# Attention's first keys, values and mask table loaded during the stage before it, and the last stores of that stage awaited by one engine

## Chip, cores and metric

One Trainium2 chip, one NeuronCore. The time is that of one execution of the program on the device, in microseconds; the kernel before was run three times.

## What is computed

Two layers of a small transformer-like network on x of shape (2, 2048, 256) in float32:

```python
x = L0_attn(x)      # a second-order linear recurrence along the sequence: B_mat in, scan, C_mat out, + x * D
x = L0_ffn(x)       # products with the signs of a 256x256 matrix, scale, bias, clip to +-100
# both between layer norms and residuals
x = L1_attn(x)      # 16 heads of 16, ALiBi slopes, causal softmax(Q K^T / 4) V, then W_out
x = L1_ffn(x)       # rotary attention with 4 key/value heads for 16 query heads, then 8 experts, top 2, SwiGLU
```

Only the two causal attentions and what comes just before them matter here. The kernel runs both in one stage of 16 steps, four heads of one batch and one attention in each step.

## The kernel before

The program is a row of stages, each with its own block of instruction streams for the five engines; a block ends when all its engines have ended.

**front** (to about 85 us) loads x, normalises it and runs the recurrence. SyncE's queue loads constants too (L147 to L163), among them the mask pieces `fill` and `after`, which count on the semaphore `s_masks`.

**middle** (to 321 us) works through 8 blocks of 512 tokens, 0 to 3 of the first batch and 4 to 7 of the second (`both(blk, ...)`). For each block it projects queries, keys and values for both attentions, splits queries and keys into a high and a low part (seven tiles `part[m]`: ScalarE's `high(m)` at L797 and L800, VectorE's `low(m)` at L907 and L910), and SyncE stores everything to DRAM: rows of x (L595, L596), `part[0..3]` as `qa_parts` and `ka_parts`, values `va_tiles` (L600), `part[4..6]` as `qb_parts` and `kb_parts` (L606), and `vb_tiles` last (L609). Buffers are reused: ScalarE's `high(m)` waits on `s_pst[m]` for the store of the block before, VectorE's value copy (L942) waits on `s_vst` for `va_tiles` and `vb_tiles` of the block before. The orders of all engines are written out by hand.

The first attention step (t = 0) reads batch 0 only, so its operands are complete in DRAM after block 3. GpSimd therefore loads part of them while the middle still runs (L533 to L585): `x_rows(blk)` and `carry(blk + 1)` for the middle itself, at block 5 a wait for the stores of block 3, then one third of the queries per block (`first_queries`, six loads of 256 KB into `q0`), and at the end `first_extras` and `first_keys`, which fill `k0a`, the keys of the first 512 tokens alone (six loads of 64 KB and two of 24 KB). SyncE closes the middle with waits for all stores of all seven parts, of the rows and of the values, and for `s_first`.

**attention** (from 325 us) runs the 16 steps. Work units of a step stand in a string written by hand, `FIRST_ORDER` for step 0: `m` is a max tile (TensorE L1406, reduced by VectorE at L1574 or L1577), `r` turns a block's row maxima on TensorE (L1433), `w` copies them (ScalarE) and SyncE stores them into two rows of `q` (L1258), `s` is a score tile (L1417, masked by L1383, exponential on ScalarE L1524), `v` a value product (L1485), `t`, `d`, `o` handle the output. Step 0 begins with 17 max tiles, then `r`, `w`, one more `m`, and the first `s`. Seven PSUM banks go round among m, r, s and t tiles, so that the tile in a bank waits for the reader of the tile seven before.

At the stage's start SyncE loads the mask table `later` (256 KB, L1263) and the keys of tokens 512 to 1023, and ScalarE the keys of tokens 1024 to 2047 and the values of step 0 (1 MB). TensorE and VectorE wait for `s_masks` = 64, so for `later`; TensorE waits for the further keys where they are first used, and issues ten dense products that do nothing but keep it busy before the first `r`:

```python
            pe.wait_ge(M["s_masks"], 64)
...
                        if t == 0 and n == 2 * KEYED[0]:
                            pe.wait_ge(s_k[0], NFK)
                        if t == 0 and n == 2 * KEYED[1]:
                            pe.wait_ge(s_k[1], NFK)
...
                        if t == 0 and n == 0:
                            keep_going(pe, M, ps_o, 10)
```

The later stages (output projections, routing, experts) are not touched.

Of the kernel before, what the change touches and what calls it, by code (L numbers as in the profile page):

```python
# [9 lines left out]
F32 = mybir.dt.float32  # L10
# [3 lines left out]

P = 128
# [72 lines left out]
def front(nc, A, M):  # L88
# [5 lines left out]
    with ExitStack() as ctx:  # L94
# [47 lines left out]
        def _(sp):  # L142
# [14 lines left out]
            for dst, src in ((M["fill"], "c_fill"),  # L157
                             (M["after_q"][0], "c_after0"), (M["after_q"][1], "c_after1")):
                sp.dma_start(dst[:, :], A[src]).then_inc(M["s_masks"], 16)
# [281 lines left out]
def first_keys(eng, M, j):  # L441

    for n in range(NPROD):
        at = HALF * j + n * HD
        eng.dma_start(M["k0a"][at:at + HD, :, :].bitcast(F32),
                      M["ka_d"][PROD_K[n], 0:GH * HD, 0:BT].rearrange("(p j d) t -> j d p t", p=PAIRS, j=2)[j]
                      ).then_inc(M["s_first"], 16)
    at = HALF * j + DOTS
    eng.dma_start(M["k0a"][at:at + SLOPED + 2, :, :].bitcast(F32),
                  M["aug_d"][SLOPED:2 * SLOPED + 2, j * PAIRS:(j + 1) * PAIRS, 0:BT]).then_inc(M["s_first"], 16)  # L450


def first_extras(eng, M, j):
    at, heads = HALF * j + DOTS, slice(j * PAIRS, (j + 1) * PAIRS)
    eng.dma_start(M["q0"][at:at + SLOPED, :, :].bitcast(F32), M["aug_d"][0:SLOPED, heads, :]).then_inc(M["s_first"], 16)


def middle(nc, A, M):

    with ExitStack() as ctx:  # L460
# [68 lines left out]
        def _(pool):  # L529
# [41 lines left out]
            for blk in range(2, NBLK):  # L571
# [15 lines left out]
        def _(sp):  # L587
# [3 lines left out]
            for blk in range(NBLK):  # L591
# [5 lines left out]
                for m in range(NS):  # L597
                    if m == 4:
# [8 lines left out]
                                 part[m][:, :, :].bitcast(F32)).then_inc(s_pst[m], 16)  # L607
                sp.wait_ge(s_va, blk * 2 + 2)
# [420 lines left out]
KEYED = [min(m for m in range(NMX) if MAXES[m][2][0][2] >= k0) for k0 in (WIDE, 2 * WIDE)]  # L1029
# [63 lines left out]
def attention(nc, A, M):  # L1093
# [4 lines left out]
    with ExitStack() as ctx:  # L1098
# [7 lines left out]
        q_op = [M["q0"], *(sb(f"a_q{i}", [P, PAIRS, L], F32R) for i in range(1, 3))]  # L1106
        v_op = [sb(f"a_v{i}", [P, KT, GH * VW]) for i in range(3)]
        prob = sb("a_p", [P, NPB, QB])
        fill, after_q = M["fill"], M["after_q"]
        later = sb("a_later", [P, WIDE])  # L1110
# [9 lines left out]
        numbers = sb("a_numbers", [P, TOK // P])  # L1120
        raw_w = sb("a_raww", [P, WIDE], F32R)
        high_w = sb("a_highw", [P, WIDE], F32R)
        k_op = [sb(f"a_k{i}", [P, PAIRS, L], F32R) for i in (0, 2, 1)]
        k_op = [k_op[0], k_op[2], k_op[1]]
# [6 lines left out]
        s_k = [sem(f"att_first_keys_loaded{i}") for i in range(2)]  # L1131
        s_v = [sem(f"att_values_loaded{i}") for i in range(5)]
# [23 lines left out]
        DIRECT = 2  # L1156
        TOPS = NQB - DIRECT
# [76 lines left out]
        NFK = (2 * NPROD + 2) * 16  # L1234

        def first_step_keys(eng, done, lo, hi):

            for j in range(2):
                for n in range(NPROD):
                    at = HALF * j + n * HD  # L1240
                    eng.dma_start(k_op[0][at:at + HD, :, lo:hi].bitcast(F32),
                                  M["ka_d"][PROD_K[n], 0:GH * HD, lo:hi].rearrange(
                                      "(p j d) t -> j d p t", p=PAIRS, j=2)[j]).then_inc(done, 16)
                at = HALF * j + DOTS
                eng.dma_start(k_op[0][at:at + SLOPED + 2, :, lo:hi].bitcast(F32),
                              M["aug_d"][SLOPED:2 * SLOPED + 2, j * PAIRS:(j + 1) * PAIRS, lo:hi]).then_inc(done, 16)

# [3 lines left out]
        def _(sp):  # L1251
# [11 lines left out]
            sp.dma_start(later[:, :], A["c_later"]).then_inc(M["s_masks"], 16)  # L1263
            first_step_keys(sp, s_k[0], BT, 2 * BT)
# [25 lines left out]
        def _(pool):  # L1290
            pool.sem_inc(s_mp, MP0)
            nc.gpsimd.memset(zeros[:, :, :], 0.0).then_inc(s_hi, 1)
            pool.dma_start(numbers[:, :], A["c_ids"]).then_inc(s_zs, 16)
            pool.wait_ge(s_hi, 1)
            pool.wait_ge(s_zs, 16)
# [41 lines left out]
            def step(t):  # L1337
# [3 lines left out]
                for what, h in work_of(t):  # L1341
# [7 lines left out]
                    elif t == 0 and what == "max" and n % 5 == 0 and 0 <= n // 5 - 4 < len(LOADS):  # L1349
                        pool.wait_ge(s_mt, 2 * n)  # L1350
# [14 lines left out]
            pool.wait_ge(s_zs, 16 + HSROWS // P // FILL * 16)  # L1365
# [3 lines left out]
        def _(pe):  # L1369
            pe.sem_inc(s_tt, TT0)  # L1370
            pe.sem_inc(s_rt, RT0)
            pe.wait_ge(M["s_masks"], 64)
# [14 lines left out]

            def keys_of(r, k0):

                return M["k0a"] if r == 0 and k0 < BT else k_op[r % 3]  # L1390
# [9 lines left out]
            def max_half(r, n, bank):  # L1400
# [3 lines left out]
                for p, qt, k0, w, col in MAXES[n // 2 % NMX][2]:  # L1404
                    kp = 0 if r >= NGB else p
                    ins = pe.matmul(ps[bank][:, col:col + w], q_op[r % 3][part, p, qt * P:(qt + 1) * P],  # L1406
                                    keys_of(r, k0)[part, kp, k0:k0 + w], start=True, stop=True)
                ins.then_inc(s_mt, 1)

            def score_half(r, n, bank):  # L1410
# [4 lines left out]
                for p, kt, c0, w, col in tiles:  # L1415
                    kp = 0 if r >= NGB else p
                    ins = pe.matmul(ps[bank][:, col:col + w], keys_of(r, kt * P)[part, kp, kt * P:(kt + 1) * P],  # L1417
# [19 lines left out]
            def step(t):  # L1437
                o = t % 3
                for what, n in work_of(t):
                    bank = BANKS[t].get((what, n))  # L1440
                    if what == "max":
                        if t == 0 and n == 2 * KEYED[0]:
                            pe.wait_ge(s_k[0], NFK)
                        if t == 0 and n == 2 * KEYED[1]:
                            pe.wait_ge(s_k[1], NFK)
# [5 lines left out]
                    elif what == "rows":  # L1451
                        if t == 0 and n == 0:
# [1068 lines left out]
```

## Time and profile before

| | |
|---|---|
| three runs | 2369.0, 2370.15, 2374.59 us; median 2370.15 us |
| the profiled execution | 2369.36 us, its span 2367.5 us |
| TensorE busy | 2178.2 us, 92% of the span |
| VectorE busy | 2031.6 us, 86% |
| ScalarE busy | 1546.6 us, 65% |
| GpSimd busy | 674.4 us, 28% |
| mean granted TensorE clock | 0.962 of full speed |

Times in the rows are microseconds from the start of the span. PE is TensorE, PEld its weight loads, DVE VectorE, ACT ScalarE, POOL GpSimd, SP SyncE; a q behind the name (SPq) marks an instruction that issues a DMA. "[11.80 <-DMA ...]" is the idle time of the engine before the row, and what ended it. PEclk is the granted TensorE clock, 1.00 for 2.4 GHz and 0.50 for 1.2 GHz. A DMA share is the mean busy share of the 16 DMA engines (it can read a little above 1).

### The profile page before, as it was taken

The numbers are of one execution on the slowest core, as the hardware profiler recorded it, in microseconds if no ns is written. First come the engines' busy times: TensorE is split into PE (matmuls) and PEld (weight loads), VectorE is DVE, ScalarE is ACT, GpSimd is POOL, SyncE is SP. The second block draws the span as 40 slices with busy tenths as digits, with TensorE's granted clock in tenths as the row PEclk, the third lists the DMA queues.
The fourth block names the chain that finished last, engine by engine and source line by source line (L and its number), as shares of the span: only waits on it lengthen the run. The fifth ranks groups of instructions, "written<-read, shape, count | busy, mean of one in ns | idle before, by whom it ended". The sixth has DMA issues, their size and how long they took to land. (4 is left out here: it accounts for less than half of the span.)

```text
span 2367.5 us, 47823 instructions
## 1 busy us (share of the span) xinstructions
PE 2178.2 (92%) x15794; PEld 1265.1 (53%) x15795; DVE 2031.6 (86%) x5155; ACT 1546.6 (65%) x3005; POOL 674.4 (28%) x999
## 2 busy tenths in 40 slices
PE   4599968999999999999999999999998885999997
PEld 2355544444444444444444444444444653888886
DVE  7799958999999999999999999999991664777775
ACT  3144414678888888888888888888886542455443
POOL 5523002232322322322322322322111353333333
PEclk8799977999999999999999999999999996999999
DMA  4179875664554554342442442443133885444443
GB/s 168 58 221 266 275 172 80 115 123 89 103 109 89 100 112 89 82 91 66 82 90 66 83 89 66 83 88 75 53 89 108 292 280 200 81 82 80 80 80 69
DMA packets 176844, 273.63 MB, mean 116 GB/s; under 512 B 53656, under 2 KB 126504, under 8 KB 170804
## 3 DMA queue, kind: packets, MB, share of 16 engines
q0 software_dynamic: 45984, 137.68, 28.7%
q1 hardware_dynamic: 125620, 123.13, 17.3%
q10 hardware_dynamic: 5044, 10.32, 1.5%
q8 instruction: 109, 1.79, 0.3%
q14 instruction: 87, 0.71, 0.1%
HBM read 128.77 MB, written 141.24 MB: 114 GB/s over the span
## 5 line engine op out<-in xcount | busy, mean ns | idle before, releaser
L1524 ACT ACTIVATE a_p<-banks 128x512 f32<-128x512 f32 x2176 | 1131.3, 609 | 257.1 <-PE banks L1417 206.5
L1577 DVE TENSOR_REDUCE a_mx<-banks 128x1 f32<-128x512 f32 x1536 | 944.1, 682 | 19.1 <-PE banks L1406 19.0
L1485 PE MATMUL banks<-a_p,a_v 128*32 128x512 f32 (+3 forms) x5120 | 588.9, 544 | 1.5 <-ACT a_o L1542 1.1
L1406 PE MATMUL banks<-a_k,a_q 52*128 52x512 f32 (+5 forms) x1600 | 446.8, 413 | 1.9 <-DVE a_rowtop L1574 0.3
L1417 PE MATMUL banks<-a_q,a_k 50*128 50x512 f32 (+7 forms) x1600 | 415.9, 396 | 1.1
L1574 DVE CUSTOM_DVE_ANT_0 a_masked<-banks,a_later 128x512 bf16<-128x512 f32 (+3 forms) x768 | 331.0, 485 | 20.3 <-PE banks L1406 18.4
L1417 PEld LDWEIGHTS banks<-a_q,a_k 54*128 54x128 f32 (+1 forms) x1600 | 227.1, 185 | 199.0 <-DVE a_mx L1577 95.6
L1406 PEld LDWEIGHTS banks<-a_k,a_q 52*128 52x128 f32 (+1 forms) x1600 | 224.1, 185 | 117.9 <-DVE a_mx L1577 55.4
L1406 PE MATMUL banks<-a_k,q 48*128 48x512 f32 (+6 forms) x896 | 256.5, 419 | 6.1 <-DMA a_k<-aug_rows 4.6
L1417 PE MATMUL banks<-q,a_k 50*128 50x512 f32 (+7 forms) x896 | 231.2, 400 | 1.2 <-DVE a_orow L1597 0.3
L1485 PEld LDWEIGHTS banks<-a_p,a_v 128*32 128x32 f32 x5120 | 109.3, 108 | 175.0 <-issue 125.9
L2173 POOL DMA_INDIRECT out_rows<-e_y,e_token x72 | 113.2, 1572 | 260.3 <-DMA out_rows<-e_y,e_token 218.2
L1417 PEld LDWEIGHTS banks<-q,a_k 50*128 50x128 f32 (+1 forms) x896 | 125.1, 187 | 115.4 <-DVE a_mx L1577 46.4
L2207 PE MATMUL banks<-w,e_hT 128*128 x576 | 170.6, 398 | 3.1 <-DVE e_hT L2315 3.1
L1406 PEld LDWEIGHTS banks<-a_k,q 48*128 48x128 f32 (+1 forms) x896 | 128.9, 189 | 71.1 <-DVE a_mx L1577 30.1
L1383 PE MATMUL banks<-fill,after 64*128 64x128 bf16 (+1 forms) x1280 | 132.2, 213 | 0.0
L1574 DVE CUSTOM_DVE_ANT_0 a_masked<-banks,a_later,a_mx 128x384 bf16<-128x384 f32 (+3 forms) x256 | 127.4, 545 | 2.5 <-PE banks L1406 2.1
L2281 ACT ACTIVATE e_w<-w 128x1024 fp32r x72 | 76.4, 1061 | 77.5 <-PE banks L2227 77.4
L2227 PE MATMUL banks<-e_w,e_gT 128*128 128x256 f32 x864 | 121.4, 290 | 0.7 <-DVE e_y L2348 0.7
L2207 PEld LDWEIGHTS banks<-w,e_hT 128*128 128x128 f32 x576 | 104.2, 190 | 23.5 <-issue 4.0
L1333 POOL TENSOR_TENSOR a_mpart<-a_rowtop,a_zeros 128x16 fp32r<-128x16 f32 x64 | 14.6, 229 | 341.3 <-DVE a_rowtop L1581 320.4
L2263 ACT ACTIVATE e_hT<-banks 128x256 fp32r<-128x256 f32 x72 | 27.6, 384 | 126.0 <-PE banks L2194 99.5
(279 smaller groups left out, 2983.6 us busy)
## 6 DMA issues: line engine op xcount, KB each, us to landing
expert_rows<-a_zeros POOLq DMA_DIRECT2D x132, 258.0 KB, 5.3
a_k<-ka_parts POOLq DMA_DIRECT2D x42, 256.0 KB, 6.3
e_x<-expert_rows SPq DMA_DIRECT2D x72, 129.0 KB, 2.2
expert_rows<-e_y SPq DMA_DIRECT2D x72, 128.0 KB
qa_parts<-m_part SPq DMA_DIRECT2D x16, 512.0 KB, 6.5
ka_parts<-m_part SPq DMA_DIRECT2D x16, 512.0 KB, 5.4
va_tiles<-m_va SPq DMA_DIRECT2D x8, 1024.0 KB, 6.8
qb_parts<-m_part SPq DMA_DIRECT2D x16, 512.0 KB
```

The lines of the kernel that those rows point to most:

```text
L1383: ins[j] = pe.matmul(blocks[:, :, HALF * n:HALF * (n + 1)], steps[n][half, :], fill[half, :].unsqueeze(1).to_broadcast([HALF, len(at), HALF]),
L1406: ins = pe.matmul(ps[bank][:, col:col + w], q_op[r % 3][part, p, qt * P:(qt + 1) * P], keys_of(r, k0)[part, kp, k0:k0 + w], start=True, st ...
L1417: ins = pe.matmul(ps[bank][:, col:col + w], keys_of(r, kt * P)[part, kp, kt * P:(kt + 1) * P], q_op[r % 3][part, p, qb * QB + c0:qb * QB + ...
L1485: ins = pe.matmul(ps_o[VW * h:VW * h + VW, c0:c0 + w], v_op[o][:, kt, hk * VW:hk * VW + VW], prob[:, (at + slot) % NPB, col:col + w], star ...
L1524: nc.scalar.activation(prob[:, (t * NSC + n) % NPB, :], ps[bank][:, :], ACT.Exp, scale=SCALE).then_inc(s_ex, 1)
L1574: ins = v.tensor_tensor_reduce(masked[:, j, col:col + w], ps[bank][:, col:col + w], later[:, WIDE - w:WIDE], 1.0, least, ALU.add, ALU.max, ...
L1577: ins = v.tensor_reduce(top, ps[bank][:, :], AX.X, ALU.max)
L2173: pool.indirect_dma_start(out=out, out_offset=bass.IndirectOffsetOnAxis(ap=token[n % R][:, :], axis=0), in_=y[n % R][:, :], in_offset=None ...
L2207: ins = pe.matmul(bank[:, :], hT[c][s][:, k, :], of[:, ds(at, 1), part * FFN:(part + 1) * FFN].rearrange("p o m -> p (o m)"), start=(k == ...
L2227: ins = pe.matmul(ps_y[:, 0:D], gT[c][s][:, f, :], w2p[of][s][:, f, :], start=(f == 0 and c == 0 and of == 0), stop=(f == FT - 1 and c == 1))
L2263: nc.scalar.activation(hT[0][s][:, :, :].rearrange("p k t -> p (k t)"), ps_h[:, 0:D], ACT.Copy).then_inc(s_hi, 1)
L2281: nc.scalar.activation(w2p[0][s][:, :, :], w2[:, ds(e * FT, FT), :], ACT.Copy)
```

## The change

Batch 0's half of `xnT` and of `f2` are no longer read once block 3 has gone through, and the full keys (`k0`, 2 MB) and the values (`v0`, 1 MB) of step 0 are placed there. `first_keys` loads full keys by thirds beside the queries, `first_values` is a new load in SyncE's queue before the last store of block 5, `later` and `numbers` are loaded in front. The loads at attention's start, the waits on `s_k` and the dense products before the first `r` are gone. The middle no longer waits for its last stores of parts and values; GpSimd does, before its first load for step 1.

```diff
             for dst, src in ((M["fill"], "c_fill"),
+                             (M["later"], "c_later"), (M["numbers"], "c_ids"),
                              (M["after_q"][0], "c_after0"), (M["after_q"][1], "c_after1")):
                 sp.dma_start(dst[:, :], A[src]).then_inc(M["s_masks"], 16)
...
-def first_keys(eng, M, j):
-    for n in range(NPROD):
-        at = HALF * j + n * HD
-        eng.dma_start(M["k0a"][at:at + HD, :, :].bitcast(F32),
-                      M["ka_d"][PROD_K[n], 0:GH * HD, 0:BT].rearrange("(p j d) t -> j d p t", p=PAIRS, j=2)[j]
-                      ).then_inc(M["s_first"], 16)
...
+def first_keys(eng, M, j, n):
+    at = HALF * j + n * HD
+    eng.dma_start(M["k0"][at:at + HD, :, :].bitcast(F32),
+                  M["ka_d"][PROD_K[n], 0:GH * HD, :].rearrange("(p j d) t -> j d p t", p=PAIRS, j=2)[j]
+                  ).then_inc(M["s_first"], 16)
+
+def first_values(eng, M):
+    eng.dma_start(M["v0"][:, :, :], M["va_d"].rearrange("(k p) c -> p k c", p=P)[:, 0:KT, 0:GH * VW]
+                  ).then_inc(M["s_first_values"], 16)
...
 def first_extras(eng, M, j):
...
+    eng.dma_start(M["k0"][at:at + SLOPED + 2, :, :].bitcast(F32),
+                  M["aug_d"][SLOPED:2 * SLOPED + 2, heads, :]).then_inc(M["s_first"], 16)
...
                 if blk == NBB + 1:
-                    for m in range(2):
+                    for m in range(4):
                         pool.wait_ge(s_pst[m], NBB * 16 + 16)
                 if blk > NBB:
                     for j in range(2):
                         first_queries(pool, M, j, blk - NBB - 1)
+                        first_keys(pool, M, j, blk - NBB - 1)
             for j in range(2):
                 first_extras(pool, M, j)
-                first_keys(pool, M, j)
...
+                if blk == NBB + 1:
+                    sp.wait_ge(s_vst, NBB * 32 + 16)
+                    first_values(sp, M)
                 sp.wait_ge(s_va, blk * 2 + 2)
                 sp.dma_start(vb_d[:, blk * TPB:(blk + 1) * TPB, :],
                              vb[:, :, :, :].rearrange("p j h c -> p j (h c)")).then_inc(s_vst, 16)
-            for m in range(NS):
-                sp.wait_ge(s_pst[m], NBLK * 16 + 16)
             for i in range(2):
                 sp.wait_ge(s_st[i], NBLK // 2 * 32 + 16)
-            sp.wait_ge(s_vst, NBLK * 32 + 16)
             sp.wait_ge(M["s_first"], NFIRST)
+            sp.wait_ge(M["s_first_values"], 16)
...
-            sp.dma_start(later[:, :], A["c_later"]).then_inc(M["s_masks"], 16)
-            first_step_keys(sp, s_k[0], BT, 2 * BT)
...
-            first_step_keys(act, s_k[1], 2 * BT, L)
-            load(act, 0, ("values", 0, 0))
...
+                        if n // 5 == 4:
+                            for done, count in zip(M["s_moved"], M["moved"]):
+                                pool.wait_ge(done, count)
                         pool.wait_ge(s_mt, 2 * n)
                         load(pool, 1, LOADS[n // 5 - 4])
...
-                        if t == 0 and n == 2 * KEYED[0]:
-                            pe.wait_ge(s_k[0], NFK)
-                        if t == 0 and n == 2 * KEYED[1]:
-                            pe.wait_ge(s_k[1], NFK)
...
-                        if t == 0 and n == 0:
-                            keep_going(pe, M, ps_o, 10)
```

Waits for `s_masks` = 64 become waits for 80. In attention the buffers are laid out anew, so that `k0` and `v0` keep their places and the others go around them.

## Rows read from the trace of the kernel before

**Rows 1.** The page: busy time of each engine and its share of the span

```profile
PE 2178.2 (92%) x15794; PEld 1265.1 (53%) x15795; DVE 2031.6 (86%) x5155; ACT 1546.6 (65%) x3005; POOL 674.4 (28%) x999
```

**Rows 2.** Busy time by stretch, from the middle's end into attention's first step

```profile
318.00:321.50 3.50, 0.27 (x3) 0.08 (x1) 1.66 (x4) 0.63 (x1) 0.00 (x0) 1.00 0.43 135
...
321.50:345.30 23.80, 10.63 (x38) 7.54 (x39) 11.37 (x45) 0.00 (x0) 1.69 (x5) 0.50 0.84 147
345.30:352.20 6.90, 3.92 (x31) 2.48 (x31) 2.36 (x4) 2.96 (x4) 0.00 (x0) 0.99 0.01 2
352.20:365.90 13.70, 13.68 (x66) 7.12 (x64) 12.29 (x36) 3.25 (x6) 0.38 (x1) 0.50 0.00 1
...
386.30:444.40 58.10, 52.16 (x351) 24.11 (x350) 53.03 (x141) 31.24 (x60) 16.83 (x30) 0.94 0.72 118
```

**Rows 3.** Timeline of SyncE's DMA queue at the end of the middle (start us, issue us)

```profile
320.24 0.79 SPq L609 DMA_DIRECT2D vb_tiles<-m_vb  x1
325.54 0.35 SPq L1263 DMA_DIRECT2D a_later<-in_c_later  x1
```

**Rows 4.** DMA issues, 290 to 345 us: size, median us from issue to landing

```profile
a_later<-in_c_later SPq DMA_DIRECT2D x1, 256.0 KB, 4.5
...
vb_tiles<-m_vb SPq DMA_DIRECT2D x1, 256.0 KB, 4.6
```

**Rows 5.** Timeline of TensorE at attention's start: start us, us, [idle before <- releaser]

```profile
330.08 6.58 PE L1406 MATMUL banks<-k0a,q 52*128 52x384 f32 x20 [11.80 <-DMA a_later<-in_c_later]
341.25 0.80 PE L1406 MATMUL banks<-a_k,q 52*128 52x384 f32 x4 [4.59 <-DMA a_k<-aug_rows]
...
342.50 3.85 PE L75 MATMUL banks<-ident 128*128 128x128 f32 x20
346.19 0.60 PE L1433 MATMUL banks<-ident,a_mpart 128*8 128x128 f32 x4
...
350.19 0.51 PE L1417 MATMUL banks<-q,k0a 54*128 54x512 f32 x2 [2.98 <-DMA q<-a_mrow]
```

**Rows 6.** Timelines of VectorE, then GpSimd, at attention's start

```profile
331.06 0.56 DVE L1574 CUSTOM_DVE_ANT_0 a_masked<-banks,a_later 128x384 bf16<-128x384 f32 x1 [11.25 <-PE banks L1406]
...
338.16 0.21 POOL L1335 TENSOR_TENSOR a_mpart<-a_rowtop,a_mpart 128x16 fp32r<-128x16 f32 x1
```

**Rows 7.** Busy time by stretch in the second half of the middle; last: clock, DMA, GB/s

```profile
217.00:220.00 3.00, 2.61 (x24) 2.61 (x25) 2.90 (x5) 2.12 (x4) 1.98 (x3) 1.00 0.98 197
223.00:226.00 3.00, 3.00 (x8) 1.33 (x7) 2.82 (x6) 2.16 (x4) 0.00 (x0) 1.00 0.69 245
226.00:265.00 39.00, 38.89 (x149) 23.19 (x148) 35.04 (x82) 17.13 (x43) 7.33 (x13) 1.00 1.04 316
...
265.00:277.00 12.00, 12.00 (x48) 6.64 (x46) 11.29 (x20) 6.67 (x12) 0.00 (x0) 1.00 0.43 141
```

**Rows 8.** Timeline of GpSimd in the middle: the first load for attention

```profile
211.01 1.05 POOL L436 DMA_DIRECT2D q<-qa_parts  x2 [28.73 <-DMA qa_parts<-m_part]
```

**Rows 9.** Timeline of VectorE in the middle: values of three blocks taken

```profile
234.84 1.41 DVE L942 TENSOR_TENSOR m_va<-banks,m_bv 128x256 f32<-128x256 f32 x4
...
259.87 1.41 DVE L942 TENSOR_TENSOR m_va<-banks,m_bv 128x256 f32<-128x256 f32 x4
...
284.91 1.41 DVE L942 TENSOR_TENSOR m_va<-banks,m_bv 128x256 f32<-128x256 f32 x4
```

**Rows 10.** Timeline of SyncE's DMA queue in the middle: the three stores before those

```profile
225.68 0.61 SPq L609 DMA_DIRECT2D vb_tiles<-m_vb  x1
...
251.28 0.52 SPq L609 DMA_DIRECT2D vb_tiles<-m_vb  x1
...
275.48 0.78 SPq L609 DMA_DIRECT2D vb_tiles<-m_vb  x1
```

**Rows 11.** DMA issues, 251 to 252 us, then 232 to 234 us: us to landing

```profile
vb_tiles<-m_vb SPq DMA_DIRECT2D x1, 256.0 KB, 7.7
...
qa_parts<-m_part SPq DMA_DIRECT2D x1, 512.0 KB, 16.5
```

More of the change, by code:

```diff
@@ L13 @@
 ds = bass.ds
+SBUF_START, SBUF_END = 16512, 229344
+F32_BYTES, BF16_BYTES = 4, 2
 P = 128
@@ L156, in _ @@
             sp.dma_start(aug[:, :], A["c_aug"]).then_inc(s_aug, 16)
-            for dst, src in ((M["fill"], "c_fill"),
+            for dst, src in ((M["fill"], "c_fill"), (M["later"], "c_later"), (M["numbers"], "c_ids"),
                              (M["after_q"][0], "c_after0"), (M["after_q"][1], "c_after1")):
@@ L1105, in attention @@
         ps, ident = M["ps"], M["ident"]
-        q_op = [M["q0"], *(sb(f"a_q{i}", [P, PAIRS, L], F32R) for i in range(1, 3))]
-        v_op = [sb(f"a_v{i}", [P, KT, GH * VW]) for i in range(3)]
+        sb("a_room_k0", [P, PAIRS, L], F32R)
+        q1 = sb("a_q1", [P, PAIRS, L], F32R)
+        sb("a_room_v0", [P, KT, GH * VW])
+        v_op = [M["v0"], *(sb(f"a_v{i}", [P, KT, GH * VW]) for i in range(1, 3))]
         prob = sb("a_p", [P, NPB, QB])
         fill, after_q = M["fill"], M["after_q"]
-        later = sb("a_later", [P, WIDE])
+        later, numbers = M["later"], M["numbers"]
         masked = sb("a_masked", [P, 2, WIDE], BF16)
@@ L1119, in attention @@
         zeros = sb("a_zeros", [P, FILL, DR])
[L1120 removed]
         raw_w = sb("a_raww", [P, WIDE], F32R)
         high_w = sb("a_highw", [P, WIDE], F32R)
[L1123 to L1124 removed]
+        q_op = [M["q0"], q1, sb("a_q2", [P, PAIRS, L], F32R)]
+        k2, k1 = sb("a_k2", [P, PAIRS, L], F32R), sb("a_k1", [P, PAIRS, L], F32R)
+        k_op = [M["k0"], k1, k2]
         ps_o = ps[RING]
@@ L1130, in attention @@
         s_q = [M["s_first"], *(sem(f"att_operands_loaded{i}") for i in range(1, 5))]
-        s_k = [sem(f"att_first_keys_loaded{i}") for i in range(2)]
-        s_v = [sem(f"att_values_loaded{i}") for i in range(5)]
+        s_v = [M["s_first_values"], *(sem(f"att_values_loaded{i}") for i in range(1, 5))]
         s_mt = sem("att_max_tile_scored")
@@ L1232, in load @@
                               va_d[:, ds(b * KT, KT), ds(g * GH * VW, GH * VW)]).then_inc(v_sem, 16)
[L1234 to L1246, printed above, removed]
         block = ctx.enter_context(nc.Block())
@@ L1371, in _ @@
             pe.sem_inc(s_rt, RT0)
-            pe.wait_ge(M["s_masks"], 64)
+            pe.wait_ge(M["s_masks"], NMASKS)
             def mask(outs, tiles, steps):
@@ L1406, in max_half @@
                     ins = pe.matmul(ps[bank][:, col:col + w], q_op[r % 3][part, p, qt * P:(qt + 1) * P],
-                                    keys_of(r, k0)[part, kp, k0:k0 + w], start=True, stop=True)
+                                    k_op[r % 3][part, kp, k0:k0 + w], start=True, stop=True)
                 ins.then_inc(s_mt, 1)
@@ L1550, in _ @@
             ch = Chain(dve, s_dve)
-            dve.wait_ge(M["s_masks"], 64)
+            dve.wait_ge(M["s_masks"], NMASKS)
             dve.sem_inc(s_te, TE0)
@@ L2406, in of_both @@
                 return early.enter_context(nc.sbuf_tensor(name, shape, dt))
-            M["k0a"] = of_both("k0a", [P, PAIRS, BT], F32R)
+            M["later"] = of_both("later", [P, WIDE], F32)
+            M["numbers"] = of_both("numbers", [P, TOK // P], F32)
             M["q0"] = of_both("q0", [P, PAIRS, L], F32R)
@@ L2412, in program @@
             M["s_masks"], M["s_first"] = nc.alloc_semaphore("masks_loaded"), nc.alloc_semaphore("first_operands")
+            M["s_first_values"] = nc.alloc_semaphore("first_values")
             with ExitStack() as first:
```

21 lines of the change are left out of this document (9 added, 12 removed).

## The prediction, before the run

> **What bounds the kernel now.** I read the page first [rows 1]: TensorE is busy for 92% of the span, VectorE for 86%, and nearly all of that is the 16 attention steps, which the change leaves alone. So I went to the only place that the diff touches, the seam between the middle and attention, and read it by stretch [rows 2]. TensorE does nothing from 318.3 us on; the granted clock is 1.00 up to 321.5 us and 0.50 (1.2 GHz) from there to 345.3 us. Then the timelines [rows 3, 5, 6]. Two waits in a row end last there. SyncE's last store (`vb_tiles`) is issued at 320.24 us and lands 4.6 us later [rows 3, 4], at 324.8; the next stage's first instruction on SyncE comes at 325.54, so the block change costs 0.7 us. That instruction is the load of the mask table, 4.5 us to land [rows 4], at 330.04, and TensorE's first max tile starts at 330.08 [rows 5]. Later come an idle stretch of 4.59 us for further keys, 3.85 us of dense filler products, and a wait for the stored row maxima; the first score tile starts at 350.19 [rows 5]. Everything after is a chain of TensorE and VectorE work in a fixed order, so what is saved before 350.19 should be saved at the end.
>
> **The seam, step by step.** (1) Stores of parts and values are no longer awaited in the middle. What ends it next is SyncE's issue of the last one, 320.24 + 0.79 = 321.03 [rows 3]; with the same 0.7 us for the change of block, attention begins at 321.7 instead of 325.5. The stores are awaited by GpSimd before its first load for step 1, at max tile 20, well past the first score, so after they have landed: nothing. (2) The mask table is already there, as are keys and values: TensorE starts at once, at 321.8, which is 8.3 us earlier than 330.08. (3) From VectorE's first tile to the first score the kernel took 350.19 - 331.06 = 19.1 us [rows 5, 6]. GpSimd had the parts of the first row maxima ready at 338.16 + 0.21, that is 7.3 us after VectorE's start [rows 6], and TensorE turned them only at 346.19, because the keys (4.59 us idle) and the filler (3.85 us) stood before it in its queue. With both gone TensorE reaches the turn when the ring of seven banks lets it issue the 17th max tile, which is after VectorE's tenth tile, at about the same 7.3 us. From the turn to the first score stay 350.19 - 346.19 = 4.0 us. So 11.4 us in place of 19.1: 7.7 us. The first of VectorE's further tiles cover most of those 4 us. The sum of the seam is 8.3 + 7.7 = 16.0 us. (4) Removing the filler also removes what preceded the short full-clock stretch of 345.3 to 352.2 [rows 2]; TensorE was busy there for 3.9 us, 0.8 of it the filler, and without it some 2 us of real work may run at half clock. Bounds 0 (it waits for the store anyway) and 2 us; I take 1. Seam: 15 us gained. (5) Two more DMAs in front (256 and 16 KB) and the reordered `s_masks` loads are under the recurrence, which uses no DMA to speak of; the removed issues of SyncE and ScalarE at attention's start kept nobody waiting. Nothing. Were the cover in front gone, the table would cost its 4.5 us [rows 4].
>
> **The price in the middle.** The loads do not vanish, they move to where DMA is busy. From 226 to 265 us the 16 DMA engines are at 1.04, full, at 316 GB/s; before that, 223 to 226, at 0.69, and afterwards, 265 to 277, at 0.43 [rows 7]. TensorE is busy for 38.9 of those 39 us and VectorE for 35.0, so a stall there is not absorbed. The new key loads are 6 x 256 + 2 x 96 KB in place of 6 x 64 + 2 x 24 KB, 1.33 MB more. Loads of this kind run slowly even alone: 197 GB/s with the engines at 0.98 in 217 to 220 us [rows 7], where they are nearly all there is. At that rate the surplus is 6.7 us of all engines; at 316 GB/s it would be 4.2. I take 6.7, the row of the same kind of load, less the 0.9 us free in 223 to 226: the backlog grows by 5.8 us. Also GpSimd's wait at 211.01 [rows 8] now includes the stores of keys, which SyncE issues after those of queries; I allow 3 us for that. With two more loads to issue at 0.5 us each [rows 8], the two middle operations queued behind, `x_rows(6)` and `carry(7)`, come some 4 us later. Their readers are two blocks away; nothing.
>
> Who waits for the backlog? VectorE's copy of values waits for the `vb_tiles` store of the block before, the last store in each block. For block 5 it was issued at 251.28 and landed 7.7 us later, at 258.98 [rows 10, 11]; the copy began at 259.87 [rows 9]. There is 0.9 us of room. With the store 5.8 us later, VectorE stalls for 4.9 us, perhaps split between this block and the one before (store issued 225.68, copy at 234.84 [rows 9, 10]). Behind VectorE's wait stand the rope of the block, and TensorE waits for that copy to free its banks. VectorE regains its own wait for TensorE after the copy, about 1 us: 4 us lost. Then the values: `first_values`, 1 MB in pieces of 512 bytes, goes into SyncE's queue right before the `vb_tiles` store of block 5 (issued 275.48; the copy that needs it at 284.91 [rows 9, 10]). That store used to be down 4.5 to 5 us after its issue, so 4.5 us of room. 1 MB at 316 GB/s is 3.3 us, at 197 it is 5.3: a stall of 0 to 1.5 us with the issue itself; I take 1. Together **5 us** lost in the middle; the bounds are 0 (all of it fits into gaps) and about 11.
>
> A row and a rule differ on how it is spread. A 512 KB store of queries issued while GpSimd's loads held the engines took 16.5 us to land [rows 11], where a load or store of the middle otherwise takes 5 to 8; it looked as if whoever had queued first was served first. The Trainium skill (DMA: Bandwidth & Descriptors, "Queues, rings and completion order") says instead that each DMA engine takes turns between the queues that have work, packet by packet. By turns, with GpSimd's packets the larger ones, SyncE's stores would crawl for as long as GpSimd has loads; that is the second rival.
>
> **Sum.** 15 - 5 = 10 us from the profiled execution's 2369.36 us: 2359.4. The median of the three runs is 0.8 us above that execution, within their spread, and I give **2359.5 us**.
>
> **Rivals.** *Transfers fit after all* (chance 0.20): the larger loads may move at the 316 GB/s of the mixed stretch, and the 12 us at 0.43 after 265 us [rows 7] speak for room; against it the full engines from 226 us. Then the seam's 15 us stand alone: 2354.4 us. *Stores held out by GpSimd's loads* (0.22): GpSimd now has 12 x 256 KB of operands, 2 x 512 KB of x and 0.33 MB of extras from about 216.5 us on, 4.5 MB, at 197 GB/s 23 us, and with the gap before `x_rows(7)` it would be done at about 243. The `vb_tiles` store issued at 225.68 then lands there and not at 230.3; the copy wanted at 234.84 stalls for 8 us. With 1.5 us for the values 9.5 us are lost: 2363.9 us. The store of 16.5 us speaks for it; against it, the store issued at 251.28 took only 7.7 us though the engines were just as full. *The clock stays down* (0.07), which ends slower: with no filler before the first `r`, step 0's thin max tiles might leave TensorE at 1.2 GHz until about 444 us. At 0.50 it did 66 products in 13.7 us (4.8 per us), in 386.3 to 444.4, near full clock, 355 in 58.1 (6.1 per us) [rows 2]; at the lower rate those 355 take 74 us in place of 58, 16 us more: 2375 us, and beyond if it lasts into step 1. It decides from the point at which the clock is still at 0.50 past 430 us. Against it, that same stretch of 386.3 to 444.4 has nearly full clock with no filler near it. The Trainium skill (TensorE: Matmul & The Clock Gate, "Part 1: The HAM clock gate") calls the throttled state the default that activity releases, which speaks against taking filler away; by it alone I would not know when the clock returns. *The change doesn't do what it says* (0.03): something else, such as late first operands, holds the block change; 2369.
>
> **Numbers.** The forecast has 0.48. About 0.3% (7 us) can be told from no change, so faster means below 2363.0. Forecast 0.42 + first rival 0.20 + the better end of the second 0.05 = 0.67 faster; slower 0.06; the rest, 0.27, the same. The forecast's own range is 2355 to 2364; the first rival with its bounds reaches down to 2351, the second with its bounds to 2367. Range 2351 to 2367.
>
> **What the changed profile would show.** Right: attention's first TensorE product 3.5 us after the middle's last one, no idle time for the table or keys, first score 11 to 12 us after VectorE's first tile; in the middle a VectorE wait of 2 to 6 us before L942 released by a DMA at block 4 or 5, blocks of 25.0 us grown by 5 in all. Wrong: no wait before L942 (first rival); one of 8 us at block 4 (second); clock 0.50 in the 400 us (third). Most would be wrong with the forecast if the middle's delay were above 8 us, or if the first score were reached later than 335 us plus that delay.

## The result, and the profile after

The changed kernel takes **2382.38 us** (median of six runs, 2379.91 to 2385.51), the kernel before in the same comparison 2371.82 us (2368.81 to 2375.6). The ratio is 1.0039 [1.0024, 1.0054]: about 0.4% slower, where I had forecast 0.45% faster. The profiled execution took 2385.51 us, its span 2383.7 us, its mean granted clock 0.953.

The page, busy time of each engine, answers to [rows 1]:

```profile
PE 2184.8 (92%) x15774; PEld 1268.6 (53%) x15775; DVE 2031.6 (85%) x5155; ACT 1547.0 (65%) x3005; POOL 673.8 (28%) x998
```

VectorE does the same work to a tenth of a microsecond, and TensorE only 6.6 us more, so the time is in waits and in the clock. For the place, I set VectorE's instructions beside each other: every kernel of this study has the same 5155 in the same order, so the k-th of one can be held against the k-th of the other. The delay of the changed kernel is +22.2 us at the end of the middle, +13.9 at attention's first max tile, +7.3 at the first tile behind the first score, +13.8 at 465 us, +14.0 at attention's end and +16.2 at the end of the program. So the middle loses 22.2 us, the seam gives back 14.9, 6.5 are lost early in step 0, 0.2 in the rest of attention and 2.2 in the stages behind it, which no kernel changes and where the profiles of this study differ from that of before by 3.8 us more to 2.7 us less. The profiled execution is 3.1 us above its median, and that of before 2.5 us below the 2371.82 of the comparison, which is why the profiles are 16.2 us apart and the medians 10.6.

**The middle.** Busy time by stretch (columns as in [rows 7]: PE, PEld, DVE, ACT, POOL, then clock, DMA share, GB/s):

```profile
218.00:224.00 6.00, 6.00 (x20) 2.96 (x20) 5.69 (x8) 2.26 (x4) 5.82 (x7) 1.00 0.96 107
232.00:240.00 8.00, 7.25 (x30) 4.55 (x28) 2.62 (x6) 2.86 (x10) 2.41 (x5) 1.00 1.03 228
240.00:250.00 10.00, 0.00 (x0) 0.00 (x0) 0.00 (x0) 0.00 (x0) 0.00 (x0) 0.64 1.07 168
```

For ten microseconds no engine computes, and the DMA engines are full at 168 GB/s. The timeline of VectorE, then of TensorE, names the wait:

```profile
258.35 1.42 DVE L959 TENSOR_TENSOR m_va<-banks,m_bv 128x256 f32<-128x256 f32 x4 [23.72 <-DMA vb_tiles<-m_vb]
...
259.15 3.78 PE L679 MATMUL banks<-m_hT,m_wb 128*128 128x512 f32 x4 [19.90 <-DVE m_va L959]
```

It is the copy of values that [rows 9] show at 234.84 us, and it waits for the store of block 3. Timeline of SyncE's queue, then the DMA issues of 225.2 to 225.5 us:

```profile
225.21 0.52 SPq L628 DMA_DIRECT2D vb_tiles<-m_vb  x1
...
227.59 23.81 SPq L622 DMA_DIRECT2D qa_parts<-m_part  x2
...
vb_tiles<-m_vb SPq DMA_DIRECT2D x1, 256.0 KB, 33.1
```

The store was issued 0.5 us earlier than before and landed 33.1 us later, at 258.3. Behind it SyncE itself sat 23.81 us in the issue of the next stores. The queues of 228 to 256 us (packets, MB, share of the 16 engines' time) show who held the engines:

```profile
q0 software_dynamic: 654, 2.95, 57.0%
q1 hardware_dynamic: 2182, 2.79, 45.9%
```

q0 is GpSimd's queue, q1 SyncE's. In 218 to 224 us q0 had them nearly alone (94.0%). The packets of that stretch:

```profile
DMA packets 126, 0.64 MB, mean 107 GB/s; under 512 B 43, under 2 KB 43, under 8 KB 54
```

72 of the 126 are of 8 KB or more: all but one of them are rows of 2048 tokens of queries and keys, 8 KB each, into 16 partitions.

**The seam.** Timelines of TensorE, VectorE, GpSimd and SyncE around attention's start answer to [rows 3, 5, 6]:

```profile
342.48 0.79 SPq L628 DMA_DIRECT2D vb_tiles<-m_vb  x1
343.93 0.53 POOL L1294 MEMSET a_zeros<- 128x516 f32 x1 [109.53 <-POOLq L476]
344.34 8.17 PE L1406 MATMUL banks<-k,q 52*128 52x384 f32 x25 [3.82 <-PEq L476]
345.01 0.56 DVE L1566 CUSTOM_DVE_ANT_0 a_masked<-banks,later 128x384 bf16<-128x384 f32 x1 [2.96 <-PE banks L1406]
352.48 1.01 PE L1433 MATMUL banks<-ident,a_mpart 128*8 128x128 f32 x4
356.92 0.80 PE L1417 MATMUL banks<-q,k 54*128 54x512 f32 x2 [2.60 <-DVE a_mx L1569]
```

The last store is issued at 343.27 and the block changes 0.66 us later; no operand is waited for; the first score comes 11.9 us after VectorE's first tile.

**Step 0's clock.** Busy time by stretch from attention's start; in the kernel before, the clock was 0.94 in 386.3 to 444.4 us [rows 2]:

```profile
345.20:399.90 54.70, 47.23 (x218) 26.46 (x216) 43.90 (x126) 18.03 (x32) 5.28 (x12) 0.50 0.29 47
399.90:465.00 65.10, 59.28 (x361) 28.73 (x359) 56.04 (x150) 34.28 (x65) 18.61 (x33) 0.82 0.67 115
```

### The profile page after: what moved, and what is told of

Same layout as the page of the kernel before. It is cut to its first block and busy times, and to the rows that moved or that the text cites. A ratio compares the mean times of both kernels' runs of the same rounds, so it can differ in the third digit from the quotient of the medians.

```text
span 2383.7 us, 47767 instructions
## 1 busy us (share of the span) xinstructions
PE 2184.8 (92%) x15774; PEld 1268.6 (53%) x15775; DVE 2031.6 (85%) x5155; ACT 1547.0 (65%) x3005; POOL 673.8 (28%) x998
## 5 line engine op out<-in xcount | busy, mean ns | idle before, releaser
L1479 PE MATMUL banks<-a_p,a_v 128*32 128x512 f32 (+3 forms) x3200 | 364.6, 539 | 0.0
L1566 DVE CUSTOM_DVE_ANT_0 a_masked<-banks,later 128x512 bf16<-128x512 f32 (+3 forms) x768 | 330.9, 485 | 12.3 <-PE banks L1406 10.5
L1406 PE MATMUL banks<-k,q 52*128 52x512 f32 (+5 forms) x960 | 278.3, 435 | 5.4 <-PEq L476 3.8
L1417 PE MATMUL banks<-q,k 54*128 54x512 f32 (+5 forms) x960 | 258.1, 416 | 10.1 <-DMA q<-a_mrow 6.3
L1479 PE MATMUL banks<-a_p,v 128*32 128x512 f32 (+3 forms) x1920 | 227.5, 558 | 1.6 <-ACT a_o L1534 1.1
L1417 PEld LDWEIGHTS banks<-q,k 54*128 54x128 f32 (+1 forms) x960 | 139.8, 194 | 138.2 <-DVE a_mx L1569 52.4
L1406 PEld LDWEIGHTS banks<-k,q 52*128 52x128 f32 (+1 forms) x960 | 142.1, 197 | 78.8 <-DVE a_mx L1569 32.8
L1566 DVE CUSTOM_DVE_ANT_0 a_masked<-banks,later,a_mx 128x384 bf16<-128x384 f32 (+3 forms) x256 | 127.2, 543 | 0.6 <-PE banks L1406 0.2
L1479 PEld LDWEIGHTS banks<-a_p,a_v 128*32 128x32 f32 x3200 | 68.1, 108 | 105.9 <-issue 79.3
```

Of the source, the lines that this page charges most:

```text
L1417: ins = pe.matmul(ps[bank][:, col:col + w], k_op[r % 3][part, kp, kt * P:(kt + 1) * P], q_op[r % 3][part, p, qb * QB + c0:qb * QB + c0 + w ...
L1479: ins = pe.matmul(ps_o[VW * h:VW * h + VW, c0:c0 + w], v_op[o][:, kt, hk * VW:hk * VW + VW], prob[:, (at + slot) % NPB, col:col + w], star ...
L1566: ins = v.tensor_tensor_reduce(masked[:, j, col:col + w], ps[bank][:, col:col + w], later[:, WIDE - w:WIDE], 1.0, least, ALU.add, ALU.max, ...
```

## The experiments

Twelve kernels, in three groups of four, each group timed against the kernel before on one chip (its medians there: 2373.51, 2369.77 and 2368.7 us). Diffs are against the changed kernel unless another is named. "Delay" is always VectorE's, against the profile of before. All of them compute the full result. Kernels of different groups are compared by their ratios.

**e1, further keys late.** Only the keys of the first 512 tokens are loaded in the middle, as before; the others at attention's start. Barrier, mask table and values stay as changed.

```diff
-                        first_keys(pool, M, j, blk - NBB - 1)
             for j in range(2):
                 first_extras(pool, M, j)
+                for n in range(NPROD):
+                    some_keys(pool, M, j, n, 0, BT, M["s_first"])
...
+                    some_keys(sp, M, j, n, BT, 2 * BT, s_k[0])
...
+                            pe.wait_ge(s_k[0], 2 * NPROD * 16)
```

> The changed kernel, but only the keys of the first 512 tokens are loaded in the middle; the others at attention's start, by SyncE and ScalarE, and waited for as in the kernel before. Values, mask table and the awaited stores stay as changed. Theory 1 (GpSimd's full key loads hold SyncE's stores out of the DMA engines): VectorE's wait of 23.7 us before its copy of values falls below 2 us and the middle ends at 321 us as before; the first score comes some 8 us earlier than in the kernel before (keys are awaited again), and with 0 to 6 us given back in step 0 the time is 2364 to 2371 us. Theory 2 (the 1 MB of values in SyncE's queue, or the new order of SyncE's waits, makes the stall): it stays above 15 us and the time is 2380 us or more.

Measured: 2365.57 us, 0.9963 [0.995, 0.9976], as theory 1 had it. The middle's delay is +0.4 us instead of +22.2, so the larger key loads are what costs the middle its time. The first score comes 9.0 us earlier than before; TensorE waits for the further keys again, as its timeline shows:

```profile
334.87 1.33 PE L1412 MATMUL banks<-k,q 52*128 52x384 f32 x5 [6.08 <-DMA k<-ka_parts]
```

**e2, values late.** The 1 MB of values goes back to attention's start.

```diff
-                if blk == NBB + 1:
-                    sp.wait_ge(s_vst, NBB * 32 + 16)
-                    first_values(sp, M)
...
+            first_values(act, M)
```

> The changed kernel with one part undone: the values of step 0 are loaded by ScalarE at attention's start instead of by SyncE in the middle. Theory 1: nothing changes, VectorE's wait before its copy of values in the fifth block stays at 22 to 25 us, the time at 2380 to 2385 us. Theory 2: the wait goes and the time falls to 2362 or below.

Measured: 2379.95 us, 1.0035 [1.0022, 1.0047], theory 1 again; the middle's delay +21.0 us. The waits of 200 to 345 us (total, count, longest):

```profile
DVE m_va L955 <- DMA vb_tiles<-m_vb: 23.0, 1, 23.0
```

The values cost the middle 1.2 us of its 22.2. One thing more: the delay is +6.0 us at the first score and +6.2 at 465 us, so this profile does not show the 6.5 us that the changed kernel's lost there, with the same work.

**e3, queries and keys a third per block.** The loads stay GpSimd's, but each third waits until the values of its block are taken.

```diff
+            def paced(n):
+                pool.wait_ge(s_va, (NBB + n) * 2 + 1)
+                for j in range(2):
+                    first_queries(pool, M, j, n)
+                    first_keys(pool, M, j, n)
```

> The changed kernel with the same loads paced: GpSimd issues each third of queries and keys (1 MB) only when VectorE has just copied the values of blocks 4, 5 and 6, so that each burst has the 16 us until the next store that anyone waits for. Same bytes, same queues. Theory 1 with the point that it is the burst that holds stores out: the middle is longer by 0 to 3 us and the time is 2356 to 2364 us. Rival (the extra bytes cost DMA time wherever they stand): the middle is longer by 5 to 10 us, 2364 to 2372 us.

Measured: 2369.66 us, 0.998 [0.9971, 0.999]. The middle's delay falls to +7.6 us. VectorE's timeline shows where the rest is:

```profile
285.70 1.42 DVE L964 TENSOR_TENSOR m_va<-banks,m_bv 128x256 f32<-128x256 f32 x4 [1.47 <-DMA vb_tiles<-m_vb]
...
314.68 1.42 DVE L964 TENSOR_TENSOR m_va<-banks,m_bv 128x256 f32<-128x256 f32 x4 [9.07 <-DMA vb_tiles<-m_vb]
```

A third is still 1 MB at a time, and the last one, with the extras, falls on block 7's wait. Spreading helps by 14.6 us of 22.2, but the middle stays longer by what the rival said (5 to 10 us), not by 0 to 3: pacing alone is not enough.

**e4, e3 with the dense products back.**

```diff
+                        if t == 0 and n == 0:
+                            keep_going(pe, M, ps_o, 10)
```

> e3_paced with the ten dense filler products before the first turned rows put back. Theory 3 (their removal leaves TensorE at 1.2 GHz for most of step 0, which gave back 6.5 us between the first score and 465 us in the changed kernel): the first score comes up to 4 us later than in e3_paced, but step 0 gives back less, and the time is 0 to 4 us below e3_paced. Rival (the clock in step 0 does not hang on the filler): 2 to 4 us above e3_paced.

Measured: 2371.84 us, 0.9988 [0.9979, 0.9997]. Against e3 the first score is 5.1 us later, 2.2 us later at 465 us, and the median 2.18 us above: by these two profiles the products win back part of their cost in clock, not all. The time is where the rival had it, 2 to 4 us above e3; the intervals of the two ratios overlap.

**e5, keys of 1024 tokens early.** e1 with `0, 2 * BT` in the middle, and SyncE's loads and TensorE's first wait gone.

```diff
-                    some_keys(pool, M, j, n, 0, BT, M["s_first"])
+                    some_keys(pool, M, j, n, 0, 2 * BT, M["s_first"])
```

> e1_keys_late with the keys of tokens 512 to 1023 loaded in the middle too (six loads of 128 KB in place of 64 KB at the end of GpSimd's middle), only tokens 1024 to 2047 at attention's start. Theory 1 (what costs is the DMA time of loads into 16 partitions, about 8 us per MB of it, where stores are waited for): 0.4 MB more costs the middle 0 to 3 us, the wait for keys goes, and the first score comes 10 to 14 us earlier than in the kernel before; at 465 us 7 to 10 us are left; time 2361 to 2366 us. Rival: the room in the middle is used up already, the stall before the copy of values is above 5 us and the time is no better than e1_keys_late.

Measured: 2358.15 us, 0.9948 [0.9937, 0.996]. The middle's delay is -0.1 us with a VectorE wait of 1.0 us, the first score 14.6 us early and the end 14.2: the seam's whole gain at no price in the middle. The time is 3 us below the range expected: step 0 gave back 0.8 us, not 3 to 4.

**e6, all keys, by SyncE.** Two key loads stand in SyncE's own queue behind the values store in each of blocks 4, 5 and 6; queries stay with GpSimd, which no longer waits for the key stores.

```diff
+                    if m == 4 and NBB <= blk < NBB + NPROD:
+                        if blk == NBB:
+                            for i in range(2, 4):
+                                sp.wait_ge(s_pst[i], NBB * 16 + 16)
+                        for j in range(2):
+                            first_keys(sp, M, j, blk - NBB)
...
-                        first_keys(pool, M, j, blk - NBB - 1)
```

> The changed kernel with the full keys loaded in the middle by SyncE's queue instead of GpSimd's: one third (2 x 256 KB) right behind the values store of blocks 4, 5 and 6; the queries by GpSimd as in the kernel before. Theory 1a (the loads into 16 partitions are slow on any queue and fill the engines): stalls before the copy of values stay, summing to 5 to 15 us over blocks 4 to 7, less than 22 us since they are spread. Theory 1b (only GpSimd's queue pushes SyncE's stores aside): stalls below 3 us in sum, time 2357 to 2364 us.

Measured: **2354.76 us, 0.9935 [0.9921, 0.995]**, the lowest ratio of the study, below those of both kernels. Theory 1a is out for this queue and pace. The middle's delay is -0.9 us with no VectorE wait for a store, the first score 15.8 us early, the end 16.6. The stretch in which the changed kernel stood still:

```profile
240.00:250.00 10.00, 10.00 (x42) 5.84 (x41) 9.32 (x16) 5.71 (x12) 0.00 (x0) 1.00 0.92 338
```

**e7, waits and mask only.** e1 with the values late and the dense products back: the original loads, with only the barrier and the mask table changed.

```diff
-                    first_values(sp, M)
...
+            first_values(act, M)
...
+                            keep_going(pe, M, ps_o, 10)
```

> The part of the change that moves no keys or values: mask table loaded in front, last stores awaited by GpSimd alone; keys beyond the first 512 tokens and the values at attention's start, filler products in place, as in the kernel before. Both theories: the middle within 1 us of before, VectorE's first tile of attention 8 us earlier. If that start only moves the wait to the keys (they are issued 4 us earlier, landing 15 us after), the first score comes 4 to 8 us earlier and the time is 3 to 8 us below before; rival: the stores still in flight and the loads get in each other's way, below 2 us of gain.

Measured: 2365.88 us, 0.9978 [0.9969, 0.9987]. Attention starts 7.5 us early (8.1 less the middle's +0.6), but the keys then stop TensorE for 5.90 us:

```profile
335.07 1.32 PE L1408 MATMUL banks<-k,q 52*128 52x384 f32 x5 [5.90 <-DMA k<-ka_parts]
336.33 3.98 PE L77 MATMUL banks<-ident 128*128 128x128 f32 x20
```

At the first score 6.0 us are left, at 465 us and at the end 2.2: the wait for keys takes 1.5 us of the gain, and 3.8 go in step 0's clock, although the dense products are in place. The medians have 3.9 us of gain.

**e8, e5 with the gap before attention filled** by 32 products instead of 20, to see whether the clock stays up.

```diff
-            keep_going(pe, M, ps[0], 20)
+            keep_going(pe, M, ps[0], 32)
```

> e5_keys_1024 with the dense products at the very end of the middle 32 instead of 20, so that TensorE is busy until attention begins. Theory 3b (the clock falls in the gap between the stages and step 0 then runs at 1.2 GHz): the clock stays at 1.00 across the gap and step 0 gives back 2 to 4 us less than in e5_keys_1024. Rival (the thin max tiles bring the clock down anyway): it falls within 10 us of attention's start and the time is that of e5_keys_1024 within 2 us.

Measured: 2360.33 us, 0.9954 [0.9941, 0.9966], 2.2 us above e5. By stretch:

```profile
318.00:327.70 9.70, 7.89 (x63) 6.67 (x61) 6.46 (x19) 0.63 (x1) 0.71 (x2) 1.00 0.74 221
327.70:351.60 23.90, 21.27 (x90) 11.31 (x90) 22.33 (x70) 6.21 (x10) 0.43 (x2) 0.50 0.15 21
```

The clock did stay at 2.4 GHz through the seam, and then fell to 1.2 GHz inside step 0 all the same, 3.5 us after attention's start. Nothing was won. That it is slower can't be put down to the products: the intervals of the ratios overlap, and 2.2 us of the profile's difference lie in the middle (+2.1 against -0.1).

The last four separate **pace from queue**: the same six key loads, by SyncE or by GpSimd, a third per block or all at block 4 (e6 is the first of the four combinations).

**e9, by GpSimd, paced.** e6 with the loads moved to GpSimd, each third behind the copy of values of blocks 4, 5 and 6; the queries and extras have been issued by then:

```diff
+            for n in range(NPROD):
+                pool.wait_ge(s_va, (NBB + n) * 2 + 1)
+                for j in range(2):
+                    first_keys(pool, M, j, n)
```

> The keys as in e6_keys_by_sync, one third (2 x 256 KB) after the values of blocks 4, 5 and 6 have been copied, but issued by GpSimd. Queries by GpSimd at the times of the kernel before. Theory 1b (GpSimd's queue is what pushes stores aside): the middle is 4 us or more longer than in e6_keys_by_sync. Theory 1c (the pace decides, 0.5 MB per block fits whatever the queue): the middle within 2 us of e6_keys_by_sync's, time 2353 to 2359 us.

Measured: 2354.27 us, 0.9946 [0.9925, 0.9967]; the middle's delay -1.8 us, no VectorE wait for a store. This is theory 1c's forecast.

**e10, by SyncE, all at block 4.** e6 with:

```diff
-                    if m == 4 and NBB <= blk < NBB + NPROD:
+                    if m == 4 and blk == NBB:
...
+                        for n in range(NPROD):
+                            for j in range(2):
+                                first_keys(sp, M, j, n)
```

> All six key loads (1.5 MB) by SyncE in a row behind the values store of block 4. Theory 1b: the middle is within 3 us of e6_keys_by_sync's. Theory 1c: the stores queued behind them come late, the middle is 5 us or more longer, and TensorE or VectorE waits on a store in block 5.

Measured: 2355.26 us (two runs), 0.994 [0.992, 0.996]; the middle's delay -0.4 us, as theory 1b had it, and against 1c: VectorE waits 2.90 us for a store, but the middle is no longer for it.

**e11, by GpSimd, all at block 4.** e9 with:

```diff
-                pool.wait_ge(s_va, (NBB + n) * 2 + 1)
+                pool.wait_ge(s_va, (NBB + 0) * 2 + 1)
```

> The same burst of 1.5 MB of keys after the copy of values of block 4, issued by GpSimd. Theory 1b: 5 us or more longer in the middle than e10_keys_by_sync_at_once. Theory 1c: the same length as there within 3 us.

Measured: 2361.45 us, 0.9958 [0.9944, 0.9972]; the middle's delay +3.7 us. Three of its eight runs lie between 2353.36 and 2354.93 and five between 2361.19 and 2364.79, so the loss isn't in every execution; the profile is of one of the five. VectorE's timeline and one stretch of e10:

```profile
260.73 1.42 DVE L965 TENSOR_TENSOR m_va<-banks,m_bv 128x256 f32<-128x256 f32 x4 [2.90 <-DMA vb_tiles<-m_vb]
...
242.00:251.00 9.00, 9.00 (x38) 5.12 (x37) 8.18 (x15) 4.35 (x8) 0.00 (x0) 1.00 1.04 355
```

and the same two of e11:

```profile
264.85 1.42 DVE L964 TENSOR_TENSOR m_va<-banks,m_bv 128x256 f32<-128x256 f32 x4 [5.48 <-DMA vb_tiles<-m_vb]
...
242.00:251.00 9.00, 9.00 (x37) 5.13 (x36) 8.45 (x16) 4.45 (x7) 0.00 (x0) 1.00 0.99 206
```

With the loads paced, the queue makes no difference that the runs can tell (e6 and e9: ratios 0.9935 and 0.9946, intervals overlapping). On SyncE's queue the pace makes none either (e6 and e10, middle -0.9 and -0.4 us). Only the burst on GpSimd's queue costs something: by the profiles 4.1 us of the middle against e10, between the 5 or more of theory 1b and the 3 at most of 1c. Between e10 and e11 the intervals of the ratios overlap, so this rests on the profiles' rows. The theory that the queue alone decides fell with e9, that the pace alone does with e10. All four keep the keys apart from the queries and behind block 4's copy of values, and the worst of them loses 3.7 us where the changed kernel lost 22.2.

**e12, e6 with the dense products back.**

```diff
+                        if t == 0 and n == 0:
+                            keep_going(pe, M, ps_o, 10)
```

> e6_keys_by_sync with the ten filler products before the first turned rows put back. If the filler is worth its time for the clock of step 0, the time is below e6_keys_by_sync's; from the pair e3_paced and e4_paced_filler I expect it 2 to 4 us above.

Measured: 2356.85 us, 0.9949 [0.9932, 0.9965], not below e6's 0.9935; the two intervals overlap, and e6 was timed in another group. TensorE's timeline has the 4.63 us that they take before the first `r`:

```profile
327.73 4.63 PE L77 MATMUL banks<-ident 128*128 128x128 f32 x20
332.16 0.91 PE L1439 MATMUL banks<-ident,a_mpart 128*8 128x128 f32 x4
```

## Why the prediction was wrong

**Step (1), the barrier: right.** 0.7 us for the change of block was forecast, 0.66 measured.

**Steps (2) and (3), mask and first score: right.** Attention's first tile came 8.3 us earlier against the middle's end, as forecast. 11.4 us from VectorE's first tile to the first score were forecast, 11.9 came. The seam's sum without the clock was 16.0 us; 14.9 came (22.2 - 7.3), and e6 has 14.9 as well (15.8 - 0.9). e7 and e1 show which part is whose: barrier and mask give 8.1 us, and the further keys, early, the rest. The one is worth something without the other: e7 still has 6.0 us at the first score.

**Step (4), the clock: forecast 1 us (0 to 2); step 0 lost 0.2 to 6.5.** The changed kernel lost 6.5 us between the first score and 465 us. The same stretch cost 0.2 us in e2, 0.4 in e10, 0.8 in e5, 1.0 in e6, but 3.6 in e3 and e11, 4.9 in e1 and 5.8 in e8. It is not the long stretch at 0.50 behind attention's start that costs the time: e6 has one as long (54.6 us) and lost 1.0 us in all, and in the changed kernel the delay had grown only from 7.3 to 7.8 us by the tile that was at 386 us in the kernel before. The rest was lost later, where the clock fell back to 0.50 in three stretches for 24 us together, the longest from 420.3 to 434.0 us; in e6 it did so for 10 us. By stretch, first e6, then the changed kernel:

```profile
322.00:376.60 54.60, 47.88 (x223) 27.11 (x221) 44.41 (x127) 18.04 (x32) 5.40 (x13) 0.50 0.29 47
...
420.30:434.00 13.70, 13.40 (x55) 7.59 (x57) 10.57 (x21) 7.82 (x16) 5.81 (x11) 0.50 0.83 140
```

Part of the rival "the clock stays down" was therefore seen, at less than half its 16 us. Whether the removed dense products have a part in it isn't settled: e7 has them and lost 3.8 us, e2 has not and lost 0.2; but e4 lost 0.7 where e3 lost 3.6. Putting them back did not pay in either pair, for they cost 5.1 and 2.7 us at the first score. What decides when the clock comes back stays open: the work of e2 and of the changed kernel in this stretch is the same but for the load of values. (The prediction says 355 products for a row that reads 351; with 351 its rival costs 15 us, not 16.)

**The price in the middle: the step that failed.** Forecast 5 us, bounds 0 to 11; measured 22.2. That GpSimd's wait would grow by 3 us and `x_rows(6)` come 4 us later was right (214.02 against 211.01, 216.06 against 212.06). Two terms were wrong.

The first is the rate, in the sentence "Loads of this kind run slowly even alone: 197 GB/s". The row of 217 to 220 us [rows 7] is not one of this kind of load. The packets of the kernel before in that stretch:

```profile
DMA packets 153, 0.59 MB, mean 197 GB/s; under 512 B 23, under 2 KB 23, under 8 KB 139
```

Only 14 of the 153 are as large as a row of queries; 116 lie between 2 and 8 KB, and belong to the x load that GpSimd had issued at 212.06 us, between the queries. Where the 8 KB rows are nearly alone, the changed kernel moved 107 GB/s at a share of 0.96. But counting packets in the trace of before would not have given me that rate. It has such a stretch too, 220 to 222 us, in which five sixths of the bytes are rows of queries:

```profile
DMA packets 67, 0.36 MB, mean 182 GB/s; under 512 B 18, under 2 KB 18, under 8 KB 29
```

A stretch of two microseconds is little: the same one in e9 reads 124 GB/s. What is new in the changed kernel is that a load of queries and one of keys into the same 16 partitions stand next to each other in GpSimd's queue, where before the neighbours were the two halves of the queries, 64 partitions apart; e3, which has the same order, reads 124 GB/s with this queue alone (244 to 248 us). Whether that neighbourhood makes the rate was not tried, so why the rate was below the forecast's stays open.

The second is the way in which the surplus was added up. I took 1.33 MB of surplus and a backlog of 5.8 us for the store of block 4, which had 0.9 us of room. But GpSimd's whole burst, 4.5 MB by the prediction's own count, kept the store of block 3 from landing. GpSimd's queue in 214 to 256 us of the changed kernel (packets, MB, share of the 16 engines' time):

```profile
q0 software_dynamic: 990, 4.52, 64.2%
```

That is 108 GB/s over those 42 us, where the forecast had 197 GB/s and 23 us; the store landed at 258.3. That is the rival *stores held out by GpSimd's loads* with its place (block 3's store, the copy due at 234.84) and its mechanism right, and its price, 8 us, mis-sized by the same 197 GB/s: the wait measured 23.72 us. I had spoken against it with the store of 7.7 us [rows 11], but SyncE's queue had the engines to itself in that microsecond (101.7% of 251 to 252 us): GpSimd's burst was over.

e1 (middle +0.4) shows that the surplus of keys is the cause; e2 (+21.0) that the values are not: they cost 1.2 us, forecast at 1. e6, e9 and e10 show that all the keys fit into the middle if they do not come together with the queries in GpSimd's queue while block 3's store is awaited: *transfers fit after all* was a true rival, for another order of the same loads.

The trace has both readings of how the engines are shared, at different times. In 228 to 256 us GpSimd's queue had 57.0% of the engines' time and SyncE's 45.9%, each with a share in every two microseconds of it: they take turns, and whoever queued first is not served first. The Trainium skill (DMA: Bandwidth & Descriptors, "Queues, rings and completion order") has this rule, and this stretch of the trace agrees with it. Two others do not. SyncE issued stores at 219.54 and from 224.21 us of the changed kernel, and in 219.6 to 226 us GpSimd's queue alone moved data; in the kernel before, GpSimd had issued the load of x at 229.62 us, and in 229.7 to 233.9 us SyncE's queue alone did, with stores most of which were issued earlier:

```profile
q0 software_dynamic: 189, 0.84, 89.9%
...
q1 hardware_dynamic: 1113, 1.29, 104.9%
```

When the one holds and when the other stays open. SyncE's store of 256 KB stood behind two of 512 KB in its own queue, and by my reading, which no run tests, these advanced by turns against slow packets, a turn lasting as long as the slow packet does.

## What to carry to other kernels

Before loads are moved into a stretch with full DMA engines, ask which awaited store lies behind the whole burst, not behind the surplus, and how much room its waiter has. Take the rate of such loads from a stretch that holds them alone, by its packets, and give it a wide margin: rows of 8 KB went at 107 to 182 GB/s in the stretches of this case. Put moved loads behind the store or the copy that someone waits for, and apart from other loads of their kind: in e6, e9 and e10 they cost the middle nothing, where the same bytes beside the queries cost 22 us. And of several waits in a row at a seam, take the next one too: barrier and mask alone gained 6.0 us at the first score, with the keys it was up to 15.8.

## What was not expected of the hardware

- SyncE's issue of two DMAs took 23.81 us at 227.59 us in the changed kernel, 21.96 of them for the first, where one takes 0.36 us at 341.47 us: in this backlog the issuing engine stood still, with all that was queued behind it.
- Loads of 8 KB rows into 16 partitions held all 16 DMA engines at 107 GB/s (changed kernel, 218 to 224 us, share 0.96), and at 182 GB/s in the kernel before (220 to 222 us), where the mostly smaller packets of the x load went at 197 GB/s (share 0.98, [rows 7]).
- The mix of the key loads and SyncE's stores moved at 355 GB/s when both were issued by SyncE, and at 206 GB/s when GpSimd issued the keys (e10, e11, 242 to 251 us), with a DMA share of 1.04 and 0.99. So the shape of a load alone doesn't set its rate. Why was not tried.
- TensorE's clock fell to 1.2 GHz 3.5 us after attention's start in e8, with TensorE idle for only 1.14 us before its first max tile, and after attention's start it stayed at 1.2 GHz for 54.6 us in the changed kernel and for 27.3 us in e2, before it rose for the first time.
